# Two-layer attention and feed-forward kernel: output projection and feed-forward head of the second layer in one stage over all batches, with rows of the late half and the split weights kept in DRAM

## What is computed

```python
x = x + _L1_xattn_ref(...)      # ends with: attn @ Wout + bout
x = x + _L1_ffn_ref(_layernorm(x), Wg, Wu, Wd, Wr, Ag, Bg, Au, Bu, Ad, Bd)
```

```python
g_lora = xf @ Ag_e.T @ Bg_e.T * SCALING
u_lora = xf @ Au_e.T @ Bu_e.T * SCALING
h = silu(gate_base + g_lora) * (up_base + u_lora)
d_delta = h @ Ad_e.T @ Bd_e.T * SCALING
```

## Time and profile before

| | |
|---|---|
| median of 3 runs | 1890.36 us (1890.24 to 1892.28) |
| the profiled execution | 1889.4 us, its span 1887.7 us |
| instructions | 27784 |
| PE busy | 1662.8 us, 88% of the span |
| DVE busy | 1107.8 us, 59% |
| ACT busy | 815.8 us, 43% |
| POOL busy | 430.1 us, 23% |

### The profile page before, as it was taken

The page is one execution under the profiler, slowest core; times in us unless marked ns, Lnnn a source line. Parts: engine busy times, 40 slices in busy tenths (PEclk is TensorE's granted clock), DMA queues, the critical chain, the costliest instruction groups (busy, mean ns, idle before and its releaser), DMA issues. The chain is left out here.

```text
span 1887.7 us, 27784 instructions
## 1 busy us (share of the span) xinstructions
PE 1662.8 (88%) x8787; PEld 1217.4 (64%) x8787; DVE 1107.8 (59%) x1999; ACT 815.8 (43%) x1304; POOL 430.1 (23%) x394
## 2 busy tenths in 40 slices
PE   6988599999578689999999896899999888999997
PEld 4766599999456533333333374677778657778785
DVE  5886522222367578888888354554555565555555
ACT  4553233333244337777777722433333324333332
POOL 1210122222357611111000000332232203232221
PEclk9999699999788869999999897999999989999998
DMA  8894045642446632222222002011110030110101
GB/s 289 327 372 158 28 171 176 257 171 74 162 151 218 181 94 65 65 63 66 69 69 69 2 0 60 22 35 29 42 42 21 1 88 22 42 42 21 42 21 45
DMA packets 135840, 182.56 MB, mean 97 GB/s; under 512 B 62560, under 2 KB 83040, under 8 KB 130864
## 3 DMA queue, kind: packets, MB, share of 16 engines
q1 hardware_dynamic: 129488, 160.65, 27.4%
q0 software_dynamic: 6240, 20.45, 3.2%
HBM read 253.41 MB, written 61.21 MB: 167 GB/s over the span
## 5 line engine op out<-in xcount | busy, mean ns | idle before, releaser
L1926 DVE TENSOR_REDUCE r_top<-r_ring 128x1 f32<-128x512 f32 x512 | 317.6, 683 | 49.7 <-PE r_ring L1823 48.4
L1909 ACT ACTIVATE r_probs<-r_st 128x1024 f32<-128x1024 f32 x256 | 247.8, 1021 | 64.3 <-PE r_st L1810 61.7
L2482 POOL TENSOR_TENSOR f_hidS<-f_work,f_hidS 128x512 fp32r<-128x512 f32 x132 | 170.7, 1293 | 418.9 <-ACT f_hidS L2442 418.9
L2599 DVE TENSOR_TENSOR f_work<-f_work,f_u 128x512 f32<-128x512 f32 x132 | 90.8, 688 | 133.4 <-PE f_u L48 74.1
L48 PE MATMUL m_bank<-w_place,m_xT 128*128 x936 | 166.0, 326 | 3.1 <-DVE m_xT L1189 3.1
L2437 ACT ACTIVATE f_work<-f_g 128x512 f32<-128x512 f32 x132 | 79.0, 598 | 182.6 <-PE f_g L56 125.5
L2442 ACT ACTIVATE f_hidS<-f_work 128x512 fp32r<-128x512 f32 x132 | 83.3, 631 | 169.0 <-DVE f_work L2599 169.0
L48 PEld LDWEIGHTS m_bank<-w_place,m_xT 128*128 128x128 f32 x936 | 151.3, 188 | 7.1 <-issue 3.8
L1844 PE MATMUL r_out<-r_probs,early_v 128*17 128x512 f32 x1024 | 135.6, 601 | 0.5 <-ACT r_probs L1909 0.4
L48 PE MATMUL f_u<-f_xnT,f_upT 128*128 128x512 f32 x528 | 131.7, 398 | 0.0
L1823 PE MATMUL r_ring<-early_slots 48*128 48x512 f32 x256 | 110.1, 490 | 22.1 <-PEq L1281 12.8
(11 more groups left out here) (345 smaller groups left out, 2967.9 us busy)
## 6 DMA issues: line engine op xcount, KB each, us to landing
w_place<-expert_split SPq DMA_DIRECT2D x72, 1408.0 KB
w_place<-expert_split SPq DMA_DIRECT2D x36, 1024.0 KB
expert_split<-w_place SPq DMA_DIRECT2D x10, 1408.0 KB, 8.8
w_place<-expert_split SPq DMA_DIRECT2D x36, 384.0 KB
early_slots<-y_rows SPq DMA_DIRECT2D x16, 512.0 KB, 6.1
k_split<-q_qk SPq DMA_DIRECT2D x32, 256.0 KB, 3.4
q_split<-q_qk SPq DMA_DIRECT2D x32, 256.0 KB, 3.1
w_raw<-in_L_ffn_down_proj SPq DMA_DIRECT2D x8, 704.0 KB, 7.1
```

The costliest lines, as they stand in the source:

```text
L1909: nc.scalar.activation(probs[k][:, 2 * pair:2 * pair + 2, :], st_ps[pair][:], ACT.Exp, scale=SCALE).then_inc(exp_done, 1)
L1926: nc.vector.reduce_max(top[g % 2][:, q, h:h + 1], ring(place(q, h))[:], AXIS_X).then_inc(max_read, 1)
L2482: nc.gpsimd.tensor_tensor(hidS[c][:, var, LO, :], hid(c, var), fp32(hidS[c][:, var, HI, :]), ALU.subtract).then_inc(hid_split, 1)
L2599: nc.vector.tensor_tensor(hid(c, var), hid(c, var), u_ps[c][:], ALU.mult).then_inc(hid_done, 1)
```

## The change

The stages behind the attention of layer 1 are built anew, and two things are moved into earlier stages.

1. `attn` is laid out as token rows. POOL writes the attention's result there directly (`normalise` in `phase_rope_attention1`), so the copy of ACT L2024 is gone. POOL also splits the output weight there, one quarter in each of four groups (`split_weight`). Some buffers of `phase_qkv1` now lie in `attn` and in the weight's buffers.
2. `phase_out_head` takes the place of `phase_out1` and of both heads. It works over batches 2, 3, 0, 1 in a software pipeline of six passes: in pass j the output projection of the j-th batch, transposes and router of the (j-1)-th, masks and low-rank rows of the (j-2)-th. The statistics are turned into scale and shift by Sqrt on ACT once for each batch, the choice of experts is made for each batch (`route`), and the masks come from a product of the transposed choice (32 rows) with a 0/1 matrix `sel` (six matmuls for each batch) instead of spread copies and transposes. POOL normalises (`normalise`) and writes all low halves of `am`.
3. Batches 2 and 3, the late half, come first: their `xnT` and `am` (2 MB each for each batch) are stored to DRAM and fetched again at the start of the second half; the late half of the masks for the tail goes to DRAM for all four batches.
4. `phase_ffn1` has 44 unrolled steps, 22 for each half. The first half prepares weights as before, and stores each tile's split weights (128 x 3840 values, 1.97 MB) to DRAM. Tile 0 is prepared in `phase_out_head`. The second half has no preparation: it fetches the split weights into two slots, front (gate and up) and back (down and low-rank) separately.
5. Tail: the sum of batches 0 and 1 (`make_delta`, `delta_rows`) lies inside steps 22 to 24; those of batches 2 and 3 stand at the end, the rows of batch 3 are stored in four DMAs.

The core of the diff:

```diff
+            def store_split(self, sp, w):
+        sp.dma_start(self.w_dram[w], fp32(self.slots[:, w % 2, :])).then_inc(self.w_out, DMA)
...
             for g in range(GROUPS):
                 if g < TILES:
                     nc.gpsimd.tensor_tensor(x[:, g, :], x[:, g, :], bout[:], ALU.add)
+                elif g < TILES + DK:
+                    split_weight(g - TILES)
                 normalise(g)
```

More of the change, by code:

```diff
@@ new lines, in phase_out_head @@
+        maskT, work, xn = first, second, wout.raw
+        late.set_raw(third)
+        free = late.slots[:, 1, :]
+        aT = free[:, 0:4 * D].rearrange("p (a h k c) -> p a h k c", a=2, h=2, k=DK)
+        hotsT = free[0:EXP_ROWS, 4 * D:4 * D + 2 * S].rearrange("q (h n) -> q h n", h=2)
+        sel = free[0:EXP_ROWS, 6 * D:6 * D + 4 * ER].rearrange("q (k c) -> q k c", k=4)
+        rl = sb("rl", [E1, S])
+        logits, shifted, rev = (sb(name, [P, TPB, E1]) for name in ("logits", "shifted", "rev"))
@@ L1991, in _, with turn @@
         @block.tensor
         def _(pe):
[L1993 to L2001, removed]
-                for t in range(TPB):
[L2003 to L2010, removed]
-                        out_product(tile - 1, t - 1)
-                out_product(b * TPB + TPB - 1, TPB - 1)
+            def turn(bank, ins, done):
+                at = 0
+                for a in ins:
+                    n_rows, n_cols = a.shape[0], a.shape[1]
+                    last = nc.tensor.transpose(bank[0:n_cols, at:at + n_rows], a, ident[0:n_rows, 0:n_rows])
+                    at += n_rows
+                last.then_inc(done, 1)
@@ L2179, in tiles @@
[L2179 to L2189 removed]
+        mask_in, acc_clear = sem("mask_in"), sem("acc_clear")
+        z_ready, z_hi, z_split, stored = sem("z_ready"), sem("z_hi"), sem("z_split"), sem("stored")
@@ L2225, in _, with prep @@
+            sp.wait_ge(stored, DMA * (B - 1 + TPB))
         @block.tensor
         def _(pe):
[L2227 to L2229 removed]
+            def prep(f, part):
                 if part == 0:
[L2232 to L2235 removed]
@@ new lines, in prep, with ring_wait, down @@
+                    pe.wait_ge(late.raw_in, (f + 1) * late.LOADS * DMA)
+                wait_count(pe, prep_split, (f - 1) * late.PARTS + part)
+                ins, _, _ = late.part(f, part)
+                for k, a in enumerate(ins):
+                    last = nc.tensor.transpose(prep_ps[:, k * P:(k + 1) * P], a, ident[:])
+                last.then_inc(prep_turned, 1)
+            def ring_wait(use):
+                wait_count(pe, y_added, use - 2)
+            def down(step, w, c):
+                pe.wait_ge(hid_split, 3 * step + 1)
+                for i in range(TPB):
+                    use = down_use(step, i)
+                    ring_wait(use)
+                    product(nc, ring(use)[:], [([hidS[c][:, 0, h, i * P:(i + 1) * P] for h in (HI, LO)],
+                                                [late.down(w, h) for h in (HI, LO)])]).then_inc(y_ready, 1)
```

1174 lines of the change are left out of this document (679 added, 495 removed).

## The result

The changed kernel takes 1909.2 us (median of 4 runs, 1907.6 to 1916.8) where the kernel before took 1891.3 beside it (4 runs, 1890.2 to 1893.1). The ratio is 1.0101, 95% interval 1.0076 to 1.0125: slower by 1%. The profiled run took 1907.57, its span is 1905.8.

A forecast was written before the change was run, and what follows sets the result against it. PE was taken to bound the two main parts, engine-to-engine chains the rest. Terms +37.4 + 66.4 - 65.0 - 27.2 - 1.2 = +10.4 gave a span of 1898.1, median 1901 us; range 1872 to 1928.

The forecast's parts named there:

- No slack in the raw loads, and a store put ahead of them: First half: raw loads already come 0.7 to 0.9 us late per tile; the 1.97 MB store goes ahead of them.
- The wait: First half, nine tiles: loads land T + 10.4 to T + 13.5 (T: turn of part 3); extra stall 5.5 us each.
- The clock: First half: after each long stall PE runs at 1.2 GHz for about 6 us, costing 2.1 us per tile (1.4 to 2.9).
- First half: Main part of the first half: nine tiles at 7.6 us, +68.4, less 2 for the first step: +66.4 us.
- The new stage: Projection and heads: walking the order of PE, ACT and DVE gave 153.6 us against 116.2, +37.4; bounds 138 and 165.
- Between the halves and second half: Stretch between the halves disappears, -65.0 us; second half without weight preparation takes 274.7 us, -27.2.
- rival 4: Start of second half: late row loads each hold PE 2 to 3 us, +10, 1911 us; chance 0.07.
- Last tail: End of the kernel: transposed masks fall away, but batch 3's mask waits behind a store: 30 us, -1.2 (-2 to +3).
- Ahead of the stage: Attention and everything before it: no change, since POOL's weight splits lie where it waits for the next group.
- The first (loads slip past): First half: raw loads slip past the store, nine tiles cost 15 us instead of 68: 1848 us; chance 0.17.
- the second (the head packs): New stage: chains fit between PE's work better, stage of 138 to 142 us, total taken 1882; chance 0.12.
- the third: First half and new stage both worse: stalls with longer half clock (91 us), head of 165, total 1935; chance 0.11.

The follow-up runs named there:

- The doses: Changed kernel with 1.05 MB of each tile's store sent earlier (half, 1888.9 us), or with each tile's split weights stored twice ahead of the loads (double, 1953.9 us).
- the filled wait: Changed kernel, but in each of nine tiles PE runs 24 matmuls that nobody reads before it waits for the raw loads: 1898.4 us, ratio 1.0018.
- the double store: Changed kernel, but each tile stores its split weights twice, both ahead of the next raw loads, 1.97 MB more per tile: 1953.9 us, ratio 1.0325.

## Why the prediction was right, point by point

1901 us were predicted for a median, 1909 came. The sign, the cause and the stage were right, and the sum was 7.7 us of span short: 2.9 in the first half, 2.4 in the new stage, 1.4 ahead of it, 1.0 in the last tail, all of one sign. Two of the terms came out well for reasons that were partly wrong, as said below.

- *No slack in the raw loads, and a store put ahead of them.* Right: it is the whole loss. Taken away alone, the change gains 3%. The waits of before were read as 0.7 to 0.9 us; in the nine tiles they are 0.70 to 1.22, 0.92 in the mean.
- *The wait.* Landing was bounded by T + 10.4 and T + 13.5; it was T + 12.2. Extra wait taken 5.5, measured 6.77 - 0.92 = 5.85. The value was drawn below the middle by the late landing of the 1 MB store, read as a share that the loads get. The doses show the price by the byte instead: the loads got nothing for free, also with two queues. By the runs the 5.85 is 5.02 for the store, nearly the whole 5.1 that it was priced at alone, and 0.83 for the later issue (a wait of 1.75 less 0.92), for which the upper bound of 7.2 had 2.0 (T + 2.2 for T + 0.2). So a share for the loads that did not exist and a later issue priced too high offset each other: that 5.5 came near 5.85 is in part luck. The Trainium skill ("DMA: Bandwidth & Descriptors", section "Queues, rings and completion order") has the rule that descriptors of one ring are consumed in order; the trace agrees in that the store was paid nearly whole, 5.02 us of 5.1. The same section says that SP and ACT have rings on the same 16 engines, which take turns between the rings by packet; the run with the store on ACT's queue agrees in that it freed nothing (6.64 against 6.77).
- *The clock.* 2.1 taken, 2.1 measured in the mean, and shown to come from the standstill by the filled wait. The size was halfway between two bounds that lay 1.5 us apart, and that it fell there is luck too: the prediction knew nothing of the cycle of three tiles.
- *First half.* 9 x 7.6 taken against 9 x 7.9; with the first step +69.3 for +66.4. The -2 for the first step comes out at -2.1 here (69.3 less 9 x 7.93) and at about -1 in the kernel with the loads first (4.4 us below before, of which 3.4 are nine waits of 0.54 for 0.92).
- *The new stage.* +39.8 for +37.4. By the pieces of the walk: start 2.0 (2.2 taken), four projections 52.6 (49.6, and the 4.7 of half clock stood apart), gaps 5.4, 18.0 and 18.5 (6.0, 16.6, 18.0), behind the last projection 58.5 (55.5), end 1.0. What was mis-sized most is that last piece: PE waited 3.79 us and then ran the low-rank rows at a low clock, 8.52 us instead of 5.7. I had laid that pass out on PE, DVE and POOL and left ACT's order out of it, where `hot_rows_hi(3)` stood behind `masked_hi(2)`. But that order is only 1.25 us of the wait: moved away it left 2.56 us of wait and low-rank rows of 7.34, and then the expert rows' low half stood on DVE behind the 2.48 us of `mask_rows(2)`. PE in the kernel after:

```profile
1213.67 1.19 PE L2235 MATMUL h_tp<-late_weights 32*128 32x512 f32 x2 [3.79 <-issue]
...
1216.50 8.52 PE L48 MATMUL h_a<-late_xnT,h_abT 128*128 128x512 f32 x24
```

- *Between the halves and second half.* -65.0 and -27.2, both exact: not one us of idle on PE, clock 1.00. The loads of the late rows cost nothing; rival 4 did not occur.
- *Last tail.* -0.2 for -1.2. The mask behind the store landed when predicted (+18.9 forecast, DVE starts at 1874.80 + 19.6).
- *Ahead of the stage.* +1.4, in code where only POOL's part differs. The first product of the new stage starts between 1074.6 and 1081.0 in the kernels of this study, whose code up to there is the same, so the 1.4 can't be put down to the change.
- *Rivals.* The first (loads slip past) falls by the waits of 6.77, the second (the head packs) by a stage of 156 and not 142, the third by that stage, not 165, and by 71 us for the nine tiles, not 91.

## What to carry to other kernels

Where one queue carries both a store that nobody waits for and a load that an engine waits for, issue the load first: the same bytes in the other order were worth 4% here. Price a transfer put ahead of a tight load by its bytes at the full rate of all engines, and add the clock that PE loses behind the standstill; a second queue did not help here, where loads and store each filled the engines. When an operation is moved, list what stands behind it in each queue that its result feeds, the queues that store the result among them.

## What the runs showed of the hardware that was not expected

- The raw loads cost nearly twice as much engine time for each byte as the store. In the quiet tile of before 0.98 MB (2144 of 3040 packets under 512 B) take 61.0% of 7 us of all 16 engines, 4.3 us, or some 230 GB/s; the store moves 408 GB/s at a share of 1.00. The share in a window as short as the transfer, not the rate, says whether there is room.
- SP's issue of the last load took 3.80 us behind the store and 1.01 without it, and behind the double store those of the last two took 3.98 and 4.04. What follows on SP in the program is put off with it.
- The cost of the low clock hardly depended on the length of the standstill: 2.2 us at 4.3, 2.1 at 6.8, 2.2 at 11.3; but 2.9 at 4.1 where the wait stood behind the up product. Behind waits of 1.2 to 1.8 us the clock stayed at 1.00; of four waits from 1.9 to 2.3 us two were followed by 0.72. From tile to tile it went round in a cycle of three (0.50, 0.66, 0.74 over 6 us) behind equal waits. A run of matmuls that nobody reads saved nearly all of it, and each tile became 1.7 us shorter in the mean.
